# Laying out the delta stage's matmul operands by step, and filling the partitions of its bias rows and of the experts' gate rows

## The reference, cut to what matters

```python
# delta rule, per head (16 heads of 8), in sequence over the tokens
state = state * exp(g_t)
v_err = (v_t - einsum('hkv,hk->hv', state, k_t)) * b_t
state = state + einsum('hk,hv->hkv', k_t, v_err)
o_t   = einsum('hkv,hk->hv', state, q_t) * scale
# q and k are silu(conv(...)) plus a small term, each scaled to unit length per head
# out = x + sigmoid(xn @ W_gate + gate_b) * (concat(norm(o), p20) @ out_W + out_b)

# experts: 8 routed (top 2) and 2 shared, of width 128
y = sum_e gate[t, e] * (silu(xn @ w1_e) * (xn @ w3_e)) @ w2_e
```

## Time and profile before

| | |
|---|---|
| median of 3 runs | 3252.28 us |
| the profiled execution's own time | 3252.81 us |
| its span, first to last instruction | 3251.6 us |
| PE, DVE, ACT, POOL busy | 92%, 77%, 64%, 26% |
| mean granted PE clock | 0.938 |
| first `moe` | about 2490 to 2637 us |
| `delta_front` | about 2641 to 2742 us |
| `delta_steps` | about 2742 to 3015 us |
| `delta_end` | about 3015 to 3100 us |
| second `moe` | about 3100 to 3246 us |

### The profile page before, as it was taken

The page is one execution under the profiler, slowest core; times in us unless marked ns, Lnnn a source line. Parts: engine busy times, 40 slices in busy tenths (PEclk is TensorE's granted clock), DMA queues, the critical chain, the costliest instruction groups (busy, mean ns, idle before and its releaser), DMA issues. The chain is left out here.

```text
span 3251.6 us, 57932 instructions
## 1 busy us (share of the span) xinstructions
PE 2992.4 (92%) x23088; PEld 1319.8 (41%) x23088; DVE 2492.1 (77%) x3275; ACT 2069.3 (64%) x3866; POOL 837.8 (26%) x976
## 2 busy tenths in 40 slices
PE   5999999979999689999998899998887978999989
PEld 1222222246666412222223566663333533444754
DVE  8999999856666599999996566668898466766244
ACT  4999999945556469999996556547674236443121
POOL 0000000022333100000001233334774712666200
PEclk7999999979999879999998899998998988999789
DMA  2000000000000100000000000000000000000000
GB/s 96 6 21 20 16 15 16 6 5 1 1 2 1 48 15 16 15 16 15 16 16 12 1 1 2 1 2 25 0 1 10 1 0 0 1 1 1 1 1 13
DMA packets 30216, 35.34 MB, mean 11 GB/s; under 512 B 13623, under 2 KB 24058, under 8 KB 29690
## 3 DMA queue, kind: packets, MB, share of 16 engines
q1 hardware_dynamic: 29754, 31.57, 3.3%
q10 hardware_dynamic: 192, 0.07, 0.0%
HBM read 19.16 MB, written 7.34 MB: 8 GB/s over the span
## 5 line engine op out<-in xcount | busy, mean ns | idle before, releaser
L420 DVE TENSOR_REDUCE max_parts<-banks 128x2 f32<-128x1024 f32 x1024 | 1169.0, 1220 | 18.8 <-PE banks L308 18.4
L510 ACT ACTIVATE probs<-banks 128x512 f32<-128x512 f32 x2048 | 1082.6, 599 | 74.1 <-PE banks L315 57.2
L308 PE MATMUL banks<-k_parts,q_parts 48*128 48x512 bf16 x2048 | 621.4, 396 | 48.4 <-DMA k_parts<-k_scratch 24.1
L315 PE MATMUL banks<-q_parts,k_parts 51*128 51x512 bf16 x2048 | 655.0, 386 | 6.6
L333 PE MATMUL banks<-probs,v_heads 128*9 128x256 f32 x8192 | 637.8, 383 | 7.5 <-ACT pv_copy L521 0.3
L315 PEld LDWEIGHTS banks<-q_parts,k_parts 51*128 51x128 bf16 x2048 | 147.9, 94 | 482.8 <-ACT probs L510 417.7
L550 POOL CAST neg_max_parts<-neg_max 128x8 bf16<-128x8 f32 x64 | 12.9, 201 | 1151.5 <-DVE neg_max L425 1151.5
L333 PEld LDWEIGHTS banks<-probs,v_heads 128*9 128x9 f32 x8192 | 123.8, 88 | 379.1 <-issue 340.4
L1495 POOL TENSOR_TENSOR state_times_c<-state,c_row 128x1024 f32<-128x1024 f32 x63 | 148.0, 2353 | 93.2 <-ACT c_row L1810 55.1
L2108 ACT ACTIVATE silu_a<-banks 128x512 f32<-128x512 f32 x80 | 47.8, 597 | 185.9 <-PE banks L1938 185.9
L1688 DVE TENSOR_TENSOR_SCAN state<-banks,state_carry,state 128x512 f32<-128x512 f32 x128 | 157.3, 1271 | 6.4 <-ACT banks L1805 4.3
(11 more groups left out here) (471 smaller groups left out, 5182.6 us busy)
## 6 DMA issues: line engine op xcount, KB each, us to landing
outT_half<-pv_copy SPq DMA_DIRECT2D x252, 16.0 KB
prob_sums<-pv_copy SPq DMA_DIRECT2D x252, 2.0 KB
q_scratch<-qk_parts SPq DMA_DIRECT2D x8, 384.0 KB, 3.9
k_scratch<-qk_parts SPq DMA_DIRECT2D x8, 384.0 KB, 2.5
k_parts<-k_scratch SPq DMA_DIRECT2D x32, 96.0 KB
q_parts<-q_scratch SPq DMA_DIRECT2D x28, 96.0 KB
k_parts<-k_scratch SPq DMA_DIRECT2D x32, 64.0 KB
q_parts<-neg_max_rows SPq DMA_DIRECT2D x128, 3.0 KB
```

The source lines that it names most:

```text
L308: nc.tensor.matmul(Mb[m % 2][:, blk(x)], Q[p % 2][half_of(x, ROWS), tile(t)], K[p % 2][half_of(x, ROWS), blk(b)], start=True, stop=True).t ...
L315: nc.tensor.matmul(bank("exp", n, x)[:, :], K[p % 2][half_of(x, ROWS + PARTS), tile(t)], Q[p % 2][half_of(x, ROWS + PARTS), blk(j)], start ...
L420: nc.vector.tensor_reduce(mxp[s % 2][:, :, u // NB, u % NB], Mb[m % 2].rearrange("p (x k) -> p x k", x=2), AX.X, ALU.max).then_inc(*maxed. ...
L510: nc.scalar.activation(PT[:, n % RING, x, :], bank("exp", n, x)[:, :], ACT.Exp, scale=float(HD) ** -0.5).then_inc(*exped.inc())
```

## The change

- Three operands of the recurrence lie step by step: column 32s + g for step s, segment g. `normalise` and `scale_keys` (the former second half of `scale_values`) write them so, into other buffers than they read (`keys_by_step` is new, queries go to the buffer `k`, scaled keys to the buffer `q`, beta to a new `nb`). The spreads read 256 adjacent columns. `scale_keys` runs behind its unit's `scale_values`, two units later, with the last two after the loop.
- `MQ` becomes `[128, HD, BATCH, 2, SEG]`: POOL writes with a stride of 256 floats between key dimensions, `sum_queries` reads 256 adjacent columns.
- `CT` times `inv` moves from POOL to DVE, between the scan and `convolve(1)`.
- ACT's silu of the values, with its two table loads, moves from ahead of the squares to behind `inverse_norm(4)`.
- `rows` has 128 partitions, zeroed by POOL as the program's first instruction; the loads write partition 0, and SyncE waits for the zeroing. The delta stage's two bias matmuls take `ones` (128 partitions) and all of `rows`; attention takes partition 0 as before.
- `moe`: the three gate parts stand at columns 0, 32 and 64 of 96 (`GATE_ROWS`), the rest zero, so `GT`, `sel` and L1943 have 96 partitions. POOL zeroes `GP` once per `moe`.

```diff
@@ moe @@
+GATE_ROWS = 32 * PARTS
-        GP, GT = sb("gate_split", [128, NT, PARTS * EXPERTS], BF16), sb("gate_parts", [PARTS * EXPERTS, N], BF16)
-        sel, falling = sb("gate_select", [PARTS * EXPERTS, EXPERTS, 128], BF16), sb("falling", [128, EXPERTS])
+        GP, GT = sb("gate_split", [128, NT, GATE_ROWS], BF16), sb("gate_parts", [GATE_ROWS, N], BF16)
+        sel, falling = sb("gate_select", [GATE_ROWS, EXPERTS, 128], BF16), sb("falling", [128, EXPERTS])
-        part = lambda k: GP[:, :, k * EXPERTS:(k + 1) * EXPERTS]
+        part = lambda k: GP[:, :, 32 * k:32 * k + EXPERTS]
+            nc.gpsimd.memset(GP[:, :, :], 0.0).then_inc(*constants.inc())
...
@@ delta_front, on_pool @@
-            pool.wait_ge(scanned, 1)
-            pool.wait_ge(cosine, 1)
-            nc.gpsimd.tensor_tensor(CT[:, :], CT[:, :], inv[:, :], ALU.mult).then_inc(*cosine.inc())
@@ delta_front, spread_row @@
-                cols = seg(source[:, :])[:, :, 0:GRP].rearrange("p g s -> p s g")
+                cols = source[:, 0:GRP * SEG]
@@ delta_front, on_dve @@
+            dve.wait_ge(scanned, 1)
+            nc.vector.tensor_tensor(CT[:, :], CT[:, :], inv[:, :], ALU.mult).then_inc(*cosine_turned.inc())
             convolve(1)
...
-                dve.wait_ge(beta_steps, beta_steps.made)
+
+            def scale_keys(b):
                 dve.wait_ge(betas_decayed, b + 1)
-                dve.wait_ge(normed, b + 1)
-                nc.vector.scalar_tensor_tensor(kn[:, blk(b)], nbd[:, blk(b)], -1.0, k[:, blk(b)], ALU.mult, ALU.mult).then_inc(*beta_steps.inc())
+                dve.wait_ge(normed, 2 * NB)
+                nc.vector.scalar_tensor_tensor(stepwise(scaled_by_step, b), in_segments(nbd, b), -1.0, stepwise(keys_by_step, b), ALU.mult, ALU.mult).then_inc(*beta_steps.inc())
...
-                nc.vector.tensor_tensor(d, d, norm[i][:, blk(b)], ALU.mult).then_inc(*normed.inc())
+                if i == 0:
+                    dve.wait_ge(normed, NB)
+                    dve.wait_ge(squares_made, NB)
+                nc.vector.tensor_tensor(stepwise(keys_by_step if i == 1 else queries_by_step, b), in_segments(dsts[i], b), in_segments(norm[i], b), ALU.mult).then_inc(*normed.inc())
@@ delta_front, on_act @@
             for n in range(1, 2 * NB):
                 square(n)
                 inverse_norm(n - 1)
+                if n == NB + 1:
+                    values()
@@ delta_steps @@
-        MQ = [sb(f"state_queries{i}", [128, BATCH, 2, SEG, HD]) for i in range(2)]
+        MQ = [sb(f"state_queries{i}", [128, HD, BATCH, 2, SEG]) for i in range(2)]
-                nc.gpsimd.tensor_tensor(MQ[s // BATCH % 2][:, s % BATCH, :, :, :], S[s % 2][:, :, :, 0:HD], kinds(QB[s // GRP % 2][:, s % GRP, :, :]), ALU.mult).then_inc(*queried.inc())
+                nc.gpsimd.tensor_tensor(MQ[s // BATCH % 2][:, :, s % BATCH, :, :].rearrange("p k x g -> p x g k"), S[s % 2][:, :, :, 0:HD], kinds(QB[s // GRP % 2][:, s % GRP, :, :]), ALU.mult).then_inc(*queried.inc())
-                cols = seg(sources[n // HD][:, :])[:, :, grp * GRP:(grp + 1) * GRP].rearrange("p g s -> p s g")
+                cols = sources[n // HD][:, grp * GRP * SEG:(grp + 1) * GRP * SEG]
-                    i = nc.tensor.matmul(o, g.ident[:, :], MQ[c % 2][:, :, :, :, kk].rearrange("p j x g -> p (j x g)"), start=(kk == 0), stop=(kk == HD - 1))
+                    i = nc.tensor.matmul(o, g.ident[:, :], MQ[c % 2][:, kk, :, :, :].rearrange("p j x g -> p (j x g)"), start=(kk == 0), stop=(kk == HD - 1))
@@ delta_end @@
-                i = nc.tensor.matmul(o, g.ones_row[:, 0:128], w["gate_b"], start=False, stop=True)
+                i = nc.tensor.matmul(o, ones[:, :], w["gate_b"], start=False, stop=True)
@@ build @@
-    g.ones_row, rows = keep("ones_row", [1, 128]), keep("row_biases_sb", [1, 2 * D])
+    g.ones_row, rows = keep("ones_row", [1, 128]), keep("row_biases_sb", [128, 2 * D])
+    nc.gpsimd.memset(rows[:, :], 0.0).then_inc(*row_zeroed.inc())
-            nc.sync.dma_start(rows[:, :], row_src[k:k + 1, :]).then_inc(*mixer_in.inc())
+            sp.wait_ge(row_zeroed, 1)
+            nc.sync.dma_start(rows[0:1, :], row_src[k:k + 1, :]).then_inc(*mixer_in.inc())
```

More of the change, by code:

```diff
@@ L1966, in turn_gates @@
                 for c in range(4):
-                    i = nc.tensor.matmul(turn_banks[b % 3][0:PARTS * EXPERTS, tile(c)], GP[:, 4 * b + c, :], g.ident_bf[:, :], start=True, stop=True)
+                    i = nc.tensor.matmul(turn_banks[b % 3][0:GATE_ROWS, tile(c)], GP[:, 4 * b + c, :], g.ident_bf[:, :], start=True, stop=True)
                 i.then_inc(*gates_turned.inc())
@@ L2150 @@
 BATCH = 4
+NB_SEG = SEG // NB
 EPS_R = 1e-6
@@ L2291, in delta @@
         ou = sb("outs", [128, 2, N])
-        delta_steps(g, selk, q, k, bv, dec, nb, KN, KB, QB, S, ou)
-        delta_end(g, w, npT, bd, q, gt, ramp, KB, QB, S[1][:, :, :, 0:HD], ou)
+        delta_steps(g, selk, by_step, bv, dec, KN, KB, QB, S, ou)
+        delta_end(g, w, npT, bd, ones, q, gt, ramp, KB, QB, S[1][:, :, :, 0:HD], ou)
 def delta_constants(g, swap, ones, bd, selk, constants):
@@ L2500, in on_dve @@
                     normalise(n - 2)
+                if n > 2 * NB + 1:
+                    scale_keys(n - 2 * NB - 2)
+            for b in range(2, NB):
+                scale_keys(b)
             for m in range(3 * HD):
@@ L2530, in on_act, with values @@
                 nc.scalar.activation(CT[:, blk(b)], CT[:, blk(b)], ACT.Exp, scale=-0.5).then_inc(*var_exp.inc())
-            nc.scalar.preload_act_table(ACT.Silu)
-            act.wait_ge(conv_steps, 3 * TAPS)
-            nc.scalar.activation(bv[:, :], bv[:, :], ACT.Silu).then_inc(*v_silued.inc())
-            nc.scalar.preload_act_table_set("natural_log_exp_and_others")
+            def values():
+                nc.scalar.preload_act_table(ACT.Silu)
+                act.wait_ge(conv_steps, 3 * TAPS)
+                nc.scalar.activation(bv[:, :], bv[:, :], ACT.Silu).then_inc(*v_silued.inc())
+                nc.scalar.preload_act_table_set("natural_log_exp_and_others")
             def square(n):
@@ L2567, in delta_front, with delta_steps @@
         on_act()
-        g.rest(beta_steps, normed, ctrl_read, cosine, copied_first, copied_on_dve, values_copied)
+        g.rest(beta_steps, normed, ctrl_read, cosine, betas_decayed, copied_first, copied_on_dve, values_copied)
         g.close(s_pool, s_pe, s_act, s_dve)
-def delta_steps(g, selk, q, k, bv, dec, kn, KN, KB, QB, S, ou):
+def delta_steps(g, selk, by_step, bv, dec, KN, KB, QB, S, ou):
     nc, pe, dve, act, pool = g.nc, g.pe, g.dve, g.act, g.pool
@@ L2764, in project @@
                     nc.tensor.matmul(o, npT[:, ts], w["out"][:, 1, :], start=False, stop=False)
-                    i = nc.tensor.matmul(o, g.ones_row[:, 0:128], w["out_b"], start=False, stop=True)
+                    i = nc.tensor.matmul(o, ones[:, :], w["out_b"], start=False, stop=True)
                 if 3 in cs:
@@ L2936, in build @@
     nc.scalar.preload_act_table_set("natural_log_exp_and_others")
-    row_1, row_2 = rows[:, 0:D], rows[:, D:2 * D]
+    row_1, row_2 = rows[0:1, 0:D], rows[0:1, D:2 * D]
     g.rest(constants, cum_made)
```

43 lines of the change are left out of this document (24 added, 19 removed).

## The result

The changed kernel takes 3132.91 us (median of 4 runs, 3127.79 to 3137.31) against 3251.19 for the kernel before (4 runs, 3245.45 to 3254.86): a ratio of 0.9637, 95% interval 0.9613 to 0.9662. One execution in this study, of `moe24`, took 5056.77 us where the others of its kernel took 3146.02 to 3149.01; it is in a slow state and is left out of the median given here.

A forecast was written before the change was run, and what follows sets the result against it. PE, slowed by strided columns, was taken to set the pace of `delta_steps`, with DVE waiting. Gains of 61 + 2 + 9 + 9 = 81 us from 3252.8 gave 3172 us, range 3156 to 3212.

The forecast's parts named there:

- the strided operands: Spreads and sums in `delta_steps`: adjacent columns bring PE below DVE's pace; gain 61 us, 63 with the last sum.
- The query: POOL's strided write of `MQ` in `delta_steps`: nothing extra, the query stays at 1.20 us.
- rivals 1 and 4: `delta_steps`: POOL pays for its strided write, 3204 (chance 0.15) or 3237 (0.04); POOL takes the whole loop, 3260 (0.03).
- rival 2: `delta_steps`: PE's pauses leave it at half clock for much of each group, above DVE; 3204, chance 0.10.
- The front: `delta_front`: 1.8 + 2.8 + 1.4 - 3 + 6 = 9 us gained, from 3 to 12.
- the silu in the middle: `delta_front`: the moved silu of the values shortens PE's first wait by 2.8 us, then costs 3.
- `CT`: `delta_front`: its product with `inv` moves from POOL to DVE, ending contention with `convolve(1)`; net gain 1.8 us.
- The last sum: 16 records behind the last query: 7.4 us becomes 5.4, between 3.5 at full clock and 7 at half; gain 2 us.
- the bias rows: `delta_end`: one-partition matmuls hold the clock down; 128 partitions gain 9 us, seven iterations at 1.49 being 10.4.
- The bound 11: `delta_end`: upper bound of the gain from bias rows on 128 partitions, in us; the lower is 0.
- the gate rows: Both `moe` stages: 96 gate rows cost nothing, as L1943 streams the same 512 columns in 384 ns; 0 us.

The follow-up runs named there:

- moe24: The changed kernel with the experts' gate rows on 24 partitions again; 3146.14 us (median of three).
- bias64: The changed kernel with the delta stage's bias matmuls on 64 partitions instead of 128; 3136.18 us.
- bias96: The changed kernel with the delta stage's bias matmuls on 96 partitions instead of 128; 3131.38 us.
- moe64: The changed kernel with the experts' gate rows on 64 partitions, parts 16 rows apart, instead of 96; 3146.54 us.
- gla64: The changed kernel with the linear attention stage's expert mask spread from 64 partitions instead of 4, added rows zero; 3124.52 us.
- bias1: The changed kernel with the delta stage's two bias matmuls on one partition again; 3159.85 us.
- rows_old: The changed kernel with gate rows on 24 partitions and bias rows on one, as in the kernel before; 3175.62 us.
- bias32: The changed kernel with the delta stage's bias matmuls on 32 partitions instead of 128; 3157.66 us.
- bias72: The changed kernel with the delta stage's bias matmuls on 72 partitions instead of 128; 3126.98 us.

## Why the prediction was wrong

**Right, and shown by undoing them:** the strided operands as what paced PE, and PE as what paced the steps (63 forecast, 65.7 measured, 65.6 back with both strides). The query writes at its own rate (1.20 us forecast and measured), so rivals 1 and 4 fall, and the step stayed at 3.04 us. Of rival 2 only the first half came true: the clock of the steps stage did fall, from 0.97 to 0.87, with PE's pauses, but DVE never waits for it.

**The front was right by luck**, 9 forecast and 8.7 measured. Its first norm starts 49.8 us in, as forecast (54.4 less 4.6). From there to the values' first add it takes 19.6 us (2682.25 to 2701.88) where 17 were forecast, since the silu in the middle costs more than 3. Behind it 8.3 were won where 6 were forecast: the 25 us taken for this part ended at 2742, but the first product of the steps starts at 2745.6, so it was 28.9 before, and it is 20.6 after. Undone one by one, the parts are worth 8.9 (the spreads' stride) and 1.3 (`CT`), and the moved silu loses 3.0, where the forecast had 2.8 less 3, about even.

**The last sum** took 7.74 us before. After, PE's timeline has

```profile
2918.57 6.78 PE L2647 MATMUL banks<-state_queries,ident 128*128 128x256 f32 x16 [5.28 <-POOL state_queries L2625]
```

That is a gain of 1.0 for a forecast of 2. PE comes out of a pause of 5.28 us, and the length is near the 7 us of a half clock. In five other profiles whose sum is the same (bias64, bias96, moe24, moe64, gla64) it took 5.10 to 5.13 us after the same pause, a gain of 2.6. So the 5.4 of the forecast lies between two lengths that both occur, and a stage of 201.4 or 203.2 us is the same kernel.

**The step that failed first: the bias rows, 9 us with bounds 0 and 11; measured 28.4.** The sign and half the mechanism were right (few partitions hold the clock down). But I priced the iteration after the change by the 2.69 us of the first one in rows 8, which itself contained one-partition matmuls: it was mostly at full clock, but its overlap was broken. The value with neither cost is 1.56; with the overlap broken and the clock kept throughout it is 2.34. And I counted seven iterations with gate projections and left out the output projection's bias matmuls. These rows show how far the gate's bias matmuls reach (first and last start) in bias1, in bias64 and in the kernel after:

```profile
L2760 PE MATMUL banks<-row_biases_sb,ones_row x32: 270/417/578, 2936.4 to 2967.0; 1*128 1x128 f32 x32
```

```profile
L2760 PE MATMUL banks<-row_biases_sb,ones x32: 272/322/373, 2922.7 to 2940.1; 64*128 64x128 f32 x32
```

```profile
L2760 PE MATMUL banks<-row_biases_sb,ones x32: 275/275/275, 2927.5 to 2939.0; 128*128 128x128 f32 x32
```

That is 30.6, 17.4 and 11.5 us. So of the 28.6, 19.1 lie there: 13.2 of clock, where I had 10.4, and 5.9 of overlap, where I had nothing. The other 9.5 lie behind them, where the output projection is: 7.4 of overlap and 2.1 of clock.

**The step that failed second: the gate rows, "free of charge"; measured 15.1 over both stages.** I compared the matmul's duration (384 ns in rows 9, 382 after) and it is indeed free. The cost was in the weight load that came late and in the start of the next matmul, which the row of a group doesn't show; the timeline of the kernel before has both:

```profile
2562.97 0.39 PE L1943 MATMUL banks<-gate_parts,gate_select 24*128 24x512 bf16 x1
2563.28 1.16 PE L1953 MATMUL banks<-ffn_weights,hidden 128*128 128x128 f32 x8
...
2562.96 0.09 PEld L1943 LDWEIGHTS banks<-gate_parts,gate_select 24*128 24x128 bf16 x1 [0.76 <-issue]
```

Behind both is one missed rival: a matmul on 64 partitions or fewer between matmuls on more breaks their overlap. It makes 28.4 us (13.3 and 15.1); the clock, priced at 9, made 15.3. Together the two steps are 34.5 us above the forecast (28.4 - 9 and 15.1) of the 36.9 by which the stages' 117.9 exceed its 81. rows_old, which has neither row edit, took 3175.62, where the forecast without its 9 for the bias rows is 3181: the rest of the sum was off by 5. The bound 11 came from the same reading as the value, so it bounded nothing.

## What to carry to other kernels

Look for matmuls on 64 or fewer partitions that stand alone between ones on more, and fill them with zero rows beyond 64: here each cost 0.3 to 0.4 us at full clock, and in the gate iterations, with 32 partitions or one, they also cost half the clock. Read the price of a PE instruction from start to start, together with when its weights are loaded, and never from its duration; and don't take a sample that contains the suspect as the value without it. Two strided operands that share one engine must be priced together: each alone seemed cheap, because the other's time had become slack.

## What had not been expected of the hardware

PE fell to half clock while its records show it busy throughout: bias32 has 0.50 with PE busy for 11.00 of 11.00 us. bias72 came to the stage alike and kept 1.00 (busy for 10.65 of 12.00 us, 2924.60 to 2936.60). bias64 had 1.00 at 5.50 of 5.50 us, with its overlap broken as in bias32, but came to the stage from another last sum. The Trainium skill, "TensorE: Matmul & The Clock Gate", section "What's actually happening", explains the gate by how busy PE has been; a plain reading of that would not put the busiest of the three at the low clock, so the measurement decides. Few partitions alone don't hold the clock down either: further on in bias1, among the output projection's one-partition matmuls, it is 1.00:

```profile
2975.00:3005.00 30.00, 27.38 (x172) 21.99 (x172) 13.25 (x40) 3.90 (x6) 2.53 (x2) 1.00 0.00 1
```

A two-input POOL operation that writes single floats 1 KB apart took 1204 ns, against 1199 for the same one with adjacent writes in the kernel before. A strided memset took 2.2 ns per element, just less than the operation's own 2.3; that the write is hidden behind the rest of the operation is argued from this and not shown.
